# The order of VectorE's work in attention, and the router's rows turned inside the output projection

## What is computed

```python
x = x + L0_xattn(layernorm(x), ctx, ctx)      # 16 heads, 4 key heads, RMS norm, rotary, causal softmax
x = x + L0_ffn(layernorm(x))                  # dense FFN, 1376 wide, with LoRA and 8 routed expert LoRAs
x = x + L1_xattn(layernorm(x), ctx)           # similarity with keys, normed rows, softmax
x = x + L1_ffn(layernorm(x))                  # 64 experts, top 8 of a softmax router, capacity 128

def L0_xattn(q, k, v):                        # out = softmax(q k^T / sqrt(32), causal) v, then @ w_out.T
def L1_xattn(p, k_v):
    kv = k_v @ W_k.T + b_k
    sim = ((p @ kv) @ kv.T) * 512 ** -0.5
    sim = (sim - mean(sim)) * rsqrt(var(sim) + 1e-6) * ln_gamma + ln_beta
    return softmax(sim)
def L1_ffn(h):
    logits = h @ router_w.T                   # then top 8, gates, gather, experts, scatter
```

## Time and profile before

| | us |
|---|---|
| median of 3 runs | 1354.61 (1350.93 to 1354.62) |
| profiled execution | 1353.49 |
| its span | 1351.7 |
| TensorE busy in the span | 1199.0 (89%) |
| VectorE, ScalarE, GpSimd busy | 746.7, 525.7, 447.2 |

### The profile page before, as it was taken

One profiled execution on the slowest core, in us unless ns is written; L12 is line 12 of the kernel. 1 busy time (PEld: TensorE's weight loads), 2 busy tenths in 40 slices (PEclk: granted clock), 3 DMA queues, 4 the chain that ended last, 5 costly groups with the idle time before them and its releaser, 6 DMA issues.

```text
span 1351.7 us, 19376 instructions
## 1 busy us (share of the span) xinstructions
PE 1199.0 (89%) x6494; PEld 877.1 (65%) x6494; DVE 746.7 (55%) x1509; ACT 525.7 (39%) x1186; POOL 447.2 (33%) x506
## 2 busy tenths in 40 slices
PE   2789999888999988899999899998469999999990
PEld 2567787666777766777866677775346666666650
DVE  6866665785688678578866847563622222222220
ACT  4774222775412377442246643221223233333320
POOL 0531334321133532113443202121035655555530
PEclk9999999989999998999999899999569999999995
DMA  8012320001233000213300013624439999999847
GB/s 281 1 60 90 117 97 33 1 32 65 104 132 111 19 1 32 104 70 127 129 1 1 32 65 117 251 98 184 178 111 332 347 362 352 357 344 352 246 54 140
DMA packets 45745, 186.98 MB, mean 138 GB/s; under 512 B 6556, under 2 KB 9628, under 8 KB 31204
## 3 DMA queue, kind: packets, MB, share of 16 engines
q1 hardware_dynamic: 30804, 146.13, 28.3%
q0 software_dynamic: 14864, 39.85, 12.9%
HBM read 155.26 MB, written 34.90 MB: 141 GB/s over the span
## 4 chain that ended last, share of the span: by engine, by line
PE 71%; DVE 15%; ACT 4%; issue 3%; DMA 3%; POOL 2%; DVEq 0%; POOLq 0%; SPq 0%; ACTq 0%
PE PS L2369 13%; PE PS L1832 10%; PE PS L1834 9%; PE PS L1833 9%; PE PS L2385 4%; PE PS L1914 3%; PE PS L2389 3%; PE PS L1933 3%; DVE NM L1344 2%; PE PS L1851 2%; PE PS L2359 2%; ACT P L850 2%; DMA WRAW<-in_ffn 1%; DVE PT L1353 1%; PE PS L2202 1%
## 5 line engine op out<-in xcount | busy, mean ns | idle before, releaser
L2369 PE MATMUL PS<-WE,XGT 128*128 128x384 f32 x512 | 194.8, 504 | 1.5 <-DVE HM L1809 0.8
L850 ACT ACTIVATE P<-PS,NM 128x512 f32<-128x512 f32 (+3 forms) x256 | 132.0, 533 | 39.0 <-DVE NM L1344 38.6
L689 POOL CAST HH<-HID 128x512 fp32r<-128x512 f32 x44 | 37.2, 846 | 324.9 <-DVE HID L1697 320.6
L1832 PE MATMUL PS<-XTH,WHI 128*128 128x512 f32 x352 | 141.3, 401 | 3.4 <-DVE WLO L1640 3.4
L969 ACT ACTIVATE WHI<-WRAW 128x1280 fp32r<-128x1280 f32 x44 | 56.0, 1274 | 217.9 <-DMA WRAW<-in_ffn 217.9
L1834 PE MATMUL PS<-XTH,WLO 128*128 128x512 f32 x352 | 138.2, 393 | 0.0
L1833 PE MATMUL PS<-XTL,WHI 128*128 128x512 f32 x352 | 138.1, 392 | 0.0
L2369 PEld LDWEIGHTS PS<-WE,XGT 128*128 128x128 f32 x512 | 88.3, 192 | 57.7 <-issue 23.4
L1914 PE MATMUL PS<-ident,P 128*128 128x128 f32 x640 | 98.7, 291 | 28.2 <-ACT P L850 6.2
L1816 DVE COPY HMT<-PS 128x256 f32<-128x256 f32 x64 | 27.2, 425 | 163.7 <-PE PS L2378 163.7
L1344 DVE TENSOR_REDUCE NM<-PS 128x2 f32<-128x1024 f32 (+2 forms) x96 | 98.7, 1039 | 27.7 <-PE PS L1841 27.4
(11 more groups left out here) (312 smaller groups left out, 2702.2 us busy)
## 6 DMA issues: line engine op xcount, KB each, us to landing
WE<-in_we SPq DMA_DIRECT2D x64, 1152.0 KB, 8.0
WRAW<-in_ffn SPq DMA_DIRECT2D x44, 1060.0 KB, 4.9
acc<-HN SPq DMA_DIRECT2D x17, 256.0 KB, 6.0
XIN<-in_x SPq DMA_DIRECT2D x4, 1024.0 KB, 5.8
out<-X SPq DMA_DIRECT2D x4, 1024.0 KB, 4.2
out<-acc POOLq DMA_DIRECT2D x1, 4096.0 KB, 22.9
hx<-HN SPq DMA_DIRECT2D x3, 1152.0 KB, 4.5
CTX<-in_ctx SPq DMA_DIRECT2D x4, 256.0 KB, 2.8
```

The costliest lines, as they stand in the source:

```text
L850: act.activation(prob(t, n), PS[:, c0:c0 + (t + 1) * P], ACT.Exp, bias=NM[:, c:c + 1], accum_out=SSUM[:, c:c + 1]).then_inc(S["p_ready"], 1)
L1832: pe.matmul(dst, a[0], b_[0], start=first, stop=False, **kw)
L2369: mm = pe.matmul(bank(2 + s % 2, 0, 2 * F1), XGT[s % 2][:, k, :], WE[s][:, k * 2 * F1:(k + 1) * 2 * F1], start=(k == 0), stop=(k == KC - 1))
```

## The change

VectorE's list of an attention pass is put in another order. In each group the maxima and the copies that free a bank come first, and the tail's steps (statistics, additions, peaks, norming) and the second part of the query columns come between or behind them; the similarity step of group 1 goes the other way, ahead of the maximum of unit 5. The statistics of group 0 end behind the next group's first maxima, and what is left of the softmax in group 2 goes there too, with the statistics of group 3 spread over that group. The 16 transposes of the normed rows leave the three banks: they stand behind the first and the second tile of the output projection, in banks 6, 7, 1 and 6, and ScalarE copies them there. The turned context goes from behind the last product with V to in front of it. The three banks are taken in another rotation, and ScalarE does one copy of turned rows before four exponentials. The edit adds three lines, so a step of L1344 stands at L1347 in the changed file. Core of the diff:

```diff
+    ROWS_BANK = (6, 7, 1, 6)
...
                 order += [("sim", 1, "d")]
-            if tail and g == G - 1:
-                order += [("xT4", 0, "a"), ("xT4", 1, "a")]
             if g < G - 1:
                 order += [("stack", g + 1, 2, "a"), ("stack", g + 1, 3, "d")]
             order += [("P", g, 1, 0, 2, "d"), ("P", g, 1, 2, 2, "a")]
-            if tail and g == G - 1:
-                order += [("xT4", 2, "a"), ("xT4", 3, "a")]
             if g < G - 1:
...
             return Ring(ALONE, (4, 5, 7), 0, 0, 0, 0)
-        return Ring(BESIDE, (7, 4, 5), a, len(ALONE) - len(BESIDE) + len(BESIDE) * a,
+        return Ring(BESIDE, (4, 5, 7), a, len(ALONE) - len(BESIDE) + len(BESIDE) * a,
                     *(turned_by(ALONE, by) - turned_by(BESIDE, by) + turned_by(BESIDE, by) * a for by in "ad"))
...
+                def output_high():
+                    act.wait_ge(S["o_ready"], 1 + G * (a + 1))
+                    act.activation(OTH[:, G - 1, :], OT[:, (G - 1) % 2, :], ACT.Copy).then_inc(S["oT_last_hi"], 1)
...
                     turned(g, 2, 1)
-                    exps(a, g, 4)
                     if tail and g == 0:
                         normed_T("xT3", 2)
+                    exps(a, g, 4)
                     if tail and g == 2:
...
                         normed_T("xT3", 3)
-                    if tail and g == 3:
-                        normed_T("xT4", 0)
-                        normed_T("xT4", 1)
                     if g < G - 1:
                         stack(g + 1, 2, QST[1])
                     if tail and g == 1:
                         exp_y(0)
                     turned(g, 1, 2, 2)
-                    if tail and g == 3:
-                        normed_T("xT4", 2)
-                        normed_T("xT4", 3)
                     if g < G - 1:
...
                 unload(G - 1)
-                act.wait_ge(S["o_ready"], 1 + G * (a + 1))
-                act.activation(OTH[:, G - 1, :], OT[:, (G - 1) % 2, :], ACT.Copy).then_inc(S["oT_last_hi"], 1)
+                if tail:
+                    for t in range(NT):
+                        act.wait_ge(S["xT4_ps"], 1 + NT * b + t + 1)
+                        act.activation(XTF[:, :, t * P:(t + 1) * P], bank(ROWS_BANK[t]).rearrange(
+                            "p (k q) -> p k q", k=KC), ACT.Copy).then_inc(S["xT4_sb"], 1)
+                        if t == 1:
+                            output_high()
+                else:
+                    output_high()
             def softmax_exp(b):
...
                         query_part(1, 1)
-                    if rows_in:
-                        n = stats_x2(b, 3)
-                        n = stats_x2(b, 0)
                     if sims:
                         weighted(of_ring("var"), "ring_d", ring_count("var"))
                     if soft:
                         y(3)
-                    if norm:
-                        n = stats_x3(b, 2)
-                        n = stats_x3(b, 3)
                     maximum(g, 3)
-                    if rows_in:
-                        n = stats_x2(b, 1)
+                    turned(g, 3, 2)
                     if soft:
                         peak(3)
-                    turned(g, 3, 2)
-                    if rows_in:
-                        n = stats_x2(b, 2)
                     if sims:
                         similarity_variances(b, of_ring("vrow")[:, 0:NT],
                                              lambda ins: sig(ins, "ring_d", ring_count("vrow")))
                     if norm:
+                        n = stats_x3(b, 1)
+                    if g > 0:
+                        normalise(g - 1)
+                    maximum(g, 4)
+                    turned(g, 2, 0)
+                    if sims:
+                        similarity_scales(b)
+                        y(0)
+                    maximum(g, 5)
+                    if g < G - 1:
+                        stack(g + 1, 1, QST[0])
+                    if rows_in:
+                        n = stats_x2(b, 3)
+                    if sims:
+                        peak(0)
+                    turned(g, 2, 2)
+                    query_part(g + 2, 0)
+                    if rows_in:
+                        n = stats_x2(b, 0)
+                    if sims:
+                        y(1)
+                    if soft:
+                        divide_y(b, 0, 2)
+                        x3(0)
+                    if norm:
+                        n = stats_x3(b, 2)
+                    if g < G - 1:
+                        stack(g + 1, 3, QST[2])
+                    turned(g, 1, 0, 2)
+                    if rows_in:
+                        n = stats_x2(b, 1)
+                    if sims:
+                        peak(1)
+                    if soft:
+                        x3(1)
+                    divisors(g)
+                    if norm:
+                        n = stats_x3(b, 3)
                         step.need(n)
                         aggregate()
                         variances(b, 5, EPS_LN)
-                    if g > 0:
-                        normalise(g - 1)
+                    turned(g, 0, 0, 4)
+                    if norm:
+                        dve.wait_ge(S["hx_stored"], 16 * (b + 1))
+                        normed(b, 5, HN, "xn4_ready")
+                    if g < G - 1:
+                        maximum(g + 1, 0)
+                        maximum(g + 1, 1)
+                    query_part(g + 2, 1)
                     if rows_in:
+                        n = stats_x2(b, 2)
                         step.need(n)
                         aggregate()
                         variances(b, 3, EPS_LN)
-                    if soft:
-                        divide_y(b, 0, 2)
-                        x3(0)
-                        x3(1)
-                    maximum(g, 4)
-                    turned(g, 2, 0)
-                    if soft:
-                        n = stats_x3(b, 0)
-                        n = stats_x3(b, 1)
-                    if norm:
-                        dve.wait_ge(S["hx_stored"], 16 * (b + 1))
-                        normed(b, 5, HN, "xn4_ready", 0, 2)
-                    maximum(g, 5)
                     if sims:
-                        similarity_scales(b)
-                        y(0)
-                    if g < G - 1:
-                        stack(g + 1, 1, QST[0])
-                    query_part(g + 2, 0)
-                    if sims:
-                        peak(0)
+                        y(2)
+                        peak(2)
                     if soft:
                         divide_y(b, 2, 4)
                         x3(2)
-                    turned(g, 2, 2)
-                    if sims:
-                        y(1)
-                    if soft:
                         x3(3)
-                    if norm:
-                        normed(b, 5, HN, "xn4_ready", 2, 4)
-                    if g < G - 1:
-                        stack(g + 1, 3, QST[2])
-                    query_part(g + 2, 1)
-                    if sims:
-                        peak(1)
-                    turned(g, 1, 0, 2)
-                    divisors(g)
-                    turned(g, 0, 0, 4)
-                    if g < G - 1:
-                        maximum(g + 1, 0)
-                        maximum(g + 1, 1)
-                    if sims:
-                        y(2)
-                        peak(2)
+                        n = stats_x3(b, 0)
                 normalise(G - 1)
...
-                def normed_T(name, ready, src, t):
-                    pe.wait_ge(S[ready], 1 + NT * b + t + 1)
-                    turns.free(pe, name, t)
-                    bk = turns.bank(name, t)
+                def normed_T(t):
+                    pe.wait_ge(S["xn4_ready"], 1 + NT * b + t + 1)
+                    if t == 0:
+                        pe.wait_ge(S["out_sb"], 1 + (a + 1) * G)
+                    if t == 3:
+                        pe.wait_ge(S["xT4_sb"], 1 + NT * b + 1)
                     for k in range(KC):
-                        mm = pe.transpose(bank(bk, k * P, (k + 1) * P), src[:, t, k * P:(k + 1) * P], ident[:, :])
-                    mm.then_inc(S["ring_ps"], 1)
+                        mm = pe.transpose(bank(ROWS_BANK[t], k * P, (k + 1) * P), HN[:, t, k * P:(k + 1) * P],
+                                          ident[:, :])
+                    mm.then_inc(S["xT4_ps"], 1)
...
-                    turns.out(pe, "xT4", NT - 1)
+                    pe.wait_ge(S["xT4_sb"], 1 + NT * (b + 1))
                     for t in range(NT):
                         for k in range(KC):
                             mm = pe.matmul(bank(1, t * E1, (t + 1) * E1), XTF[:, k, t * P:(t + 1) * P], rw[:, k, :],
                                            start=(k == 0), stop=(k == KC - 1))
                     mm.then_inc(S["lgt_ps"], 1)
+                def context_T():
+                    for t in range(NT):
```

(18 more changed lines are left out.)

4 lines of the change are left out of this document (2 added, 2 removed).

## The result

The kernel after takes **1329.12 us** (median of 4 runs, 1328.08 to 1329.86), the kernel before 1353.69 in the 4 runs beside it; the ratio is 0.9818, 95% interval 0.9801 to 0.9835. The profiled execution took 1329.86, its span 1328.0 (before 1351.7).

What follows compares the result with a forecast made beforehand. TensorE was busy 1199.0 of 1351.7 us, so only its idle time, some 150 us, could be won. Three tail passes (-11.4) and the first pass (-3.0) gave -14.4: 1339.1 us (1340.2 by median), own range 1334 to 1346, wider 1330 to 1350.

Steps and rivals of the forecast that it cites:

- first pass: First pass: two 1.49 us TensorE waits go as query columns move behind the next maxima; -3.0, bounds 0 and -3.5.
- group 0: Tail pass, group 0: three statistics go behind the copies, so a bank is freed earlier; -1.5 us, bounds 0 and 2.2.
- group 1: Tail pass, group 1: similarity step comes one maximum earlier, shortening a 0.86 us TensorE wait; -0.7, bounds 0 and 1.74.
- group 2: Tail pass, group 2: 3.0 us leave VectorE's chain, 2.6 gained at full clock, 0.8 given back; -1.8, bounds 0.5 and 3.3.
- group 3: Tail pass, group 3: ends earlier without the 16 transposes, 3.1 at full clock less 1.5 for clock; -1.6, bounds 0 and 3.1.
- projection: Output projection: 16 transposes cost +1.64, GpSimd's late split +0.5, context moved out -0.35; +1.79 with the transposes.
- the charge for the clock: Each tail pass: half-clock stretches expected again, costing 0.8 us in group 2 and 1.5 net at group 3's end.
- Rival 2: Whole kernel: no half clock at all, idle time cut into short pieces; 2.3 us more per pass, 1333.3; chance 0.12.
- Rival 1: Tail passes: half clock spreads, both stretches 6.8 us after longer idle before the product with V; 1347.7; chance 0.20.
- Rival 3: Groups 0 to 2: ScalarE's exponentials are the limit, groups give nothing, only first pass left; 1351 to 1354; chance 0.08.
- Rival 4: Before the projection: GpSimd's late split makes TensorE wait, at 7 us the kernel takes 1361; chance 0.05.
- The +0.5 charged for it: Before the projection: GpSimd's late split and VectorE's norming lose time to each other; +0.5 us, bounds 0 and 2.

Runs made afterwards that it cites:

- e12: Kernel after with two additions, their reciprocal and two statistics put back in group 2, plus 26 unread identity transposes there per tail pass; 1329.77 us.
- e2: Kernel after with the old order back in the first pass and groups 0 to 2; only group 3, projection and context stay new; 1341.65 us.
- e3: Kernel before with only the two parts of the query columns moved in the first pass; 1352.24 us.
- e1: Kernel before with VectorE's new order and ScalarE's swap in the first pass and groups 0 to 2 only; 1344.25 us.
- e5: Kernel after with 18 unread identity transposes per tail pass added in group 3 to keep TensorE busy; 1328.61 us.
- e6: Kernel after with the four context transposes of each pass back behind the last product with V; 1333.79 us.
- e10: Kernel after with group 3 reordered: GpSimd's split before the power, VectorE copying tile 2's last head, last heads before aggregates, context earlier; 1325.61 us.
- e7: Kernel after with two additions, their reciprocal and two statistics put back around the maxima of units 4 and 5 of group 2; 1334.73 us.
- e9: Kernel after with ScalarE copying the key stack and tile 2's last turned head between pairs of exponentials, groups 0 to 2 and first pass; 1328.76 us.
- e11: Kernel after with the edits of e9 and e10, plus ScalarE's second query stack copy (group 0: last turned rows too) between unit 5's exponentials; 1318.44 us.
- e4: Kernel before with 32 unread identity transposes per tail pass in TensorE's waits of groups 2 and 3; 1348.08 us.

## Why the forecast was too small

Against its own steps, by the profiled executions (before less after, 23.7 us of span):

| term | forecast | measured, passes 1, 2, 3 |
|---|---|---|
| first pass | -3.0 | -2.8 |
| group 0 | -1.5 | -1.65 (24.59 to 22.94 in the first) |
| group 1 | -0.7 | -0.50, -0.52, -0.49 |
| group 2 | -1.8 | -2.98, -1.80, -3.17 |
| group 3 | -1.6 | -3.39, -3.68, -3.26 |
| projection | +1.79 | +1.78, +3.08, +1.41 |
| last tail's end | 0 | -2.8, once |
| behind it | 0 | +0.5, once |

The projection is read from "to next" of the first table, with group 0's 1.65 added back in the first two. Of the first pass's 2.8 the context moved ahead of its product with V gave 0.4.

**The direction and the mechanism were right.** The waits of 0.86 and 1.85 us for VectorE are gone and that of 2.18 is down to 0.40. At full clock the forecast had 2.6 for group 2 and 3.1 for group 3; measured were 3.0 to 3.2 and 3.3, and the first pass, group 0, group 1 and the projection at full clock (+1.4) came within 0.4.

**The step that failed** is the charge for the clock: "so I expect a stretch at the half clock again and give 0.8 back", and "1.5 us net" in group 3. Together that was 2.3 a pass, 6.9 in all. The price of a stretch was about right: one in group 2 costs 1.28 (19.04 against 17.76) and gives 0.34 back in group 3, one on the product with V and the projection costs 1.4 to 1.7 (170.01 against e12's 168.36; 176.85 and 177.04 against 175.43), and one mostly over waits 0.4. Their number was not. I charged two in each pass, six in all; after has three, worth 0.4 + 0.9 + 1.7 = 3.0.

For group 2 the runs show what the number depends on. With the old order of its steps (before, e2, e3) the clock falls in nine passes of nine; with the new one (after, e1, e5, e6, e10) in two of fifteen; with only the steps around the maxima put back, and with them the 1.85 us wait, in three of three (e7). I had written that TensorE "then still stands idle for a time in the middle of the group". It does, 1.73 us for KST, and the clock fell behind that in one pass of three of after.

At the end of group 3 the charge of one stretch was nearer: after and e9, alike there but for ScalarE's order, have four in six passes. I had argued that TensorE has "little to do in the last 3 us before the product with V, less than before where the clock fell", and had booked the move of the context as "-0.35" only. Without that move (e6) the stage takes 1.4 to 1.9 us more. How much of that is chance is open: e7 has a stretch there in two passes and e12 in none, behind equal idle time.

Two of my bounds were wrong as well. Group 3 gave 3.3 to 3.7, outside "bounds 0 and 3.1". And for group 2 the bound was "the whole idle time", though its busy time could fall too: TensorE was busy there for 17.36 us with part of it at the half clock, and for 15.02 in after.

**The other 2.8** are no effect of the edit's waits but, as far as the traces show, luck. The end of the last tail follows a wait of 14.19 us in all fourteen profiles, and then takes 15.1 us in four of the fourteen (before, e1, e3, e11) and 11.6 to 12.3 in ten, with the same instructions. The granted clock falls during the wait in all of them. In the four the work began 10.94 to 11.12 us after the fall and ran at the half clock to its end; in the ten it began 9.24 to 10.81 us after, and the clock came back 2.8 to 4.4 us into it. So it goes with the moment at which the work begins against the fall. What sets that moment stays open; e10 and e11, with the same steps in group 3, are on either side. The unprofiled runs of before spread by 3.7 us, which may be the same thing; no trace of them was kept. It was not in the range, because I had written that the last tail "only moves".

**The rest.** By the stages in which no stretch falls a tail pass gives -1.65 - 0.50 - 3.08 - 3.33 + 1.40 = -7.2, where the forecast's terms at full clock gave -6.1: 3.2 in three passes. With 3.9 for the clock (6.9 less 3.0) and 2.8 for the last tail, less 0.2 in the first pass and 0.5 behind the last tail, that makes 9.2; the gap between the sum and the spans is 9.3.

**The rivals.** Rival 2 (no half clock, 1333.3) was nearest, though two passes still had stretches. Rival 1 fell; without the move of the context it would have been partly right (e6 has 6.8 us at the half clock at the end of group 3 in two passes). Rival 3 fell for groups 0 to 2, but ScalarE is what TensorE mostly waits for now. Rival 4 fell: the split took its 0.61 and 1.27 us with the norming beside it. It was the norming that slowed, to 3.11 us for four tiles against 1.60 and 0.99 for two and two before: the two steps that began while a part of the split ran took 0.74 and 1.54 us and ended 0.3 us behind that part, the other two 0.53 each. Of the two orders that the page SBUF — State Buffer of the Trainium skill ("Who interferes with whom") left possible, the harmless one came. The +0.5 charged for it was not paid: the projection cost the 1.64 of the transposes less the context's 0.4, within 0.2.

## What to carry to other kernels

Put the price of a stretch at the lower clock and the number of such stretches in separately: the price can be read from the trace, but the number depends on the idle time ahead of them and in part on chance, so an edit that takes that idle time away can take them too, and the case without any belongs inside the range. Work that TensorE must do anyway is well placed in the wait right ahead of a stretch that it fills wholly. And removing the wait with the largest name shortens little (0 to 0.2 us in groups 0 to 2 of e9) while the engine that releases it has the same work before the group's last handover.

## What the runs showed of the chip

- The same instruction list in three passes has the clock fall in none, one or two places of them, and groups 1 to 3 are equal to 0.03 us where it does not fall. One stretch at 0.50 lasts 3.4 or 6.8 us; its cost lay between 0.4 us (mostly over waits) and 1.7 (over work that TensorE fills).
- Transposes that compute nothing pay: 96 more of them made the kernel before 5 us faster (e4), and 78 more took 3.2 us off group 2 in three passes (e12 against e7).
- Behind an idle time of 14.19 us the half clock lasted through all 12.2 us of busy time, which had no break, in four profiles, and through only the first 2.8 to 4.4 us in ten.
- Of VectorE's norming steps, the two that began while a part of GpSimd's split ran took 0.74 and 1.54 us, the two that did not 0.53 each.
